# First attention: the context of half a pass is copied out of PSUM by ScalarE instead of VectorE

## What is computed

```python
scores = jnp.einsum('bhqd,bhkd->bhqk', q, k) / jnp.sqrt(HEAD_DIM)
scores = jnp.where(causal, scores, WHERE_CONST)
probs = jax.nn.softmax(scores, axis=-1)
ctx = jnp.einsum('bhqk,bhkd->bhqd', probs, v)
out = ctx @ Wo + bo
```

## Time and profile before

| | us |
|---|---|
| median of 3 runs (3386.05 to 3387.24) | 3386.67 |
| the profiled execution | 3384.95 |
| its span on the core | 3383.2 |
| span of the first attention, from its first exponential to the end of its last multiplication | 148.8 to 663.7 |
| one pass of it, from a copy of half 0 to the next (257.32 to 289.27) | 31.95 |

### The profile page before, as it was taken

One profiled execution on the slowest core, in us unless ns is written; L12 is line 12 of the kernel. 1 busy time (PEld: TensorE's weight loads), 2 busy tenths in 40 slices (PEclk: granted clock), 3 DMA queues, 4 the chain that ended last, 5 costly groups with the idle time before them and its releaser, 6 DMA issues. The chain is left out here.

```text
span 3383.2 us, 74549 instructions
## 1 busy us (share of the span) xinstructions
PE 2601.1 (77%) x23705; PEld 1456.7 (43%) x23705; DVE 2700.5 (80%) x8588; ACT 2383.1 (70%) x3987; POOL 2029.4 (60%) x4543
## 2 busy tenths in 40 slices
PE   3699999669654777777777777775777777758999
PEld 2233333234431444444444444443554454543444
DVE  5788888235438999999999999998999999744444
ACT  2266666533117999999999999997999999822221
POOL 3133333410117999999999999996999989640000
PEclk8699999879665777777778777877777777868999
DMA  5312211000121011001101100110110110010000
GB/s 150 94 47 53 55 49 40 14 25 26 52 63 21 2 18 18 11 9 18 18 2 18 18 12 9 18 18 2 18 18 2 18 18 2 2 33 3 7 7 10
DMA packets 115264, 85.87 MB, mean 25 GB/s; under 512 B 58153, under 2 KB 97339, under 8 KB 114875
## 3 DMA queue, kind: packets, MB, share of 16 engines
q1 hardware_dynamic: 106331, 75.20, 10.4%
q0 software_dynamic: 8192, 4.79, 0.9%
q10 hardware_dynamic: 352, 1.18, 0.1%
HBM read 54.25 MB, written 19.40 MB: 22 GB/s over the span
## 5 line engine op out<-in xcount | busy, mean ns | idle before, releaser
L1285 POOL TENSOR_TENSOR a_near<-a_side,a_z 128x1024 int32<-128x1024 int32 x512 | 968.9, 1892 | 42.6
L1181 PE MATMUL a_ST<-a_qs,a_ks 75*128 75x128 bf16 x4096 | 656.5, 249 | 397.5 <-DVE a_mask L1418 208.6
L1381 DVE MAX8 a_cand<-a_near 128x8 f32<-128x256 f32 x2048 | 810.8, 414 | 0.0
L1181 PEld LDWEIGHTS a_ST<-a_qs,a_ks 75*128 75x128 bf16 x4096 | 459.1, 114 | 564.1 <-DVE a_mask L1418 338.7
L1425 DVE TENSOR_SCALAR_CACHE_REDUCE a_z<-a_S,a_thr 128x1024 f32<-128x1024 f32 x512 | 650.2, 1270 | 33.6 <-POOL a_thr L1261 27.9
L1205 ACT ACTIVATE a_signs<-a_z,a_tiny 128x1024 bf16<-128x1024 f32 x512 | 589.6, 1152 | 73.9 <-DVE a_z L1425 72.4
L1198 ACT ACTIVATE a_signs<-a_S,search 128x1024 bf16<-128x1024 f32 x512 | 572.2, 1118 | 24.3 <-PE a_S L1136 24.2
L1220 ACT ACTIVATE a_eT<-a_ST 128x1024 f32<-128x1024 f32 x512 | 520.2, 1016 | 18.0 <-PE a_ST L1182 17.5
L776 ACT ACTIVATE a_eT<-a_ST 128x512 f32<-128x512 f32 (+3 forms) x768 | 329.2, 489 | 210.0 <-PE a_ST L761 148.6
L1136 PE MATMUL a_S<-a_ks,a_qs 72*128 72x512 bf16 x1024 | 394.4, 475 | 101.4 <-DVE a_z L1425 76.6
L880 DVE TENSOR_REDUCE a_mx<-a_S 128x1 f32<-128x512 f32 (+3 forms) x768 | 381.2, 547 | 77.3 <-PE a_S L748 67.7
(11 more groups left out here) (341 smaller groups left out, 4639.6 us busy)
## 6 DMA issues: line engine op xcount, KB each, us to landing
a_qs<-q_parts SPq DMA_DIRECT2D x174, 64.0 KB
a_ks<-k_parts SPq DMA_DIRECT2D x174, 64.0 KB
a_qs<-a_flip SPq DMA_DIRECT2D x512, 0.8 KB
q_parts<-p_qp SPq DMA_DIRECT2D x48, 128.0 KB, 1.7
k_parts<-p_kp SPq DMA_DIRECT2D x48, 128.0 KB, 1.8
a_qs<-q_parts SPq DMA_DIRECT2D x60, 96.0 KB
a_ks<-k_parts SPq DMA_DIRECT2D x60, 96.0 KB
f_w<-L_ffn_W SPq DMA_DIRECT2D x16, 256.0 KB, 2.8
```

Source lines behind the costliest of these rows:

```text
L1181: pe.matmul(ST[:, block_of], ks[:, base(hl) + kb * P:base(hl) + (kb + 1) * P], qs[:, tile(hl):tile(hl) + P], start=True, stop=False)
L1285: pool.tensor_tensor(near[:, hl % NEARS, :].bitcast(I32), side[:, one].bitcast(I32).broadcast_to([P, SEQ]), z[:, hl % H, :].bitcast(I32), ...
L1381: mm = dve.max(found[:, 8 * g:8 * g + 8], near[:, h2 % NEARS, g * SW:(g + 1) * SW])
```

## The change

The copy of `O` into `num` leaves DVE's program and enters ACT's, in the same slots: ACT makes the exponential of slot 19 (or 3), then the copy, with the same waits, then the exponential of slot 20 (or 4). The last copy of the last pass stands behind all exponentials. The operation is an `ACTIVATE` with the function Copy instead of a `tensor_copy`. Nothing else is changed.

```diff
         @block.scalar
         def _(act):
             def slot(it, p):
+                gi = p // G
                 if live(it):
-                    hf, kb, lo, hi = GROUPS[p // G]
-                    gi = p // G
+                    hf, kb, lo, hi = GROUPS[gi]
                     act.wait_ge(sturn_s, it * NB_ + (p + 1))
                     if p % G == 0 and not (isinstance(it, int) and it == 0 and gi < 4):
                         act.wait_ge(pv, it * NG + (gi - 3))
                     act.activation(eT[:, gi % 4, p % G, 0:hi - lo], ST[p % TURNED][:, 0:hi - lo], ACT.Exp, scale=SCALE0).then_inc(e_done, 1)
+                for at, hf, y in ((COPY1, 1, before(it)), (COPY0, 0, it)):
+                    if p == at and live(y):
+                        act.wait_ge(pv, NG * y + (FIRST_HALF if hf == 0 else NG))
+                        if not (isinstance(y, int) and y == 0):
+                            act.wait_ge(ctx_s, 2 * y + hf)
+                        act.activation(num[:, hf, :], O[:, :], ACT.Copy).then_inc(oc, 1)
...
             with act.Fori(1, ITERS) as it:
                 for p in range(NB_):
                     slot(it, p)
+            for p in range(COPY1 + 1):
+                slot(ITERS, p)
...
         @block.vector
...
-                for at, hf, y in ((COPY1, 1, before(it)), (COPY0, 0, it)):
-                    if p == at and live(y):
-                        dve.wait_ge(pv, NG * y + (FIRST_HALF if hf == 0 else NG))
-                        if not (isinstance(y, int) and y == 0):
-                            dve.wait_ge(ctx_s, 2 * y + hf)
-                        dve.tensor_copy(num[:, hf, :], O[:, :]).then_inc(oc, 1)
```

## The result

The changed kernel takes 3392.23 us (median of 12 runs, 3388.36 to 3394.56), the kernel before 3385.41 (12 runs, 3383.53 to 3389.42): a ratio of 1.0019, 95% interval 1.001 to 1.0028. It is some 7 us slower; 3.4 us faster was forecast. The profiled execution took 3390.81, its span is 3389.1.

What follows compares the result with a forecast made beforehand. PE was taken as the bound in the middle of the first attention, waiting 20.3 us for the copy. Terms 5.1 - 0.7 - 1.1 + 0.1 = 3.4 us, so 3386.67 - 3.4 = 3383.3 us; range 3380.2 to 3387.5.

Steps and rivals of the forecast that it cites:

- What is left, 0.04: Stages after the first attention: they start some us earlier and could see clock or DMAs fall otherwise; chance 0.04, no size.
- Copy on ACT: First attention, copy of half 0 (slot 19): 0.596 us on ACT, PE starts 0.43 us earlier, 6.5 us over fifteen places.
- Slot 3: First attention, copy of half 1: ACT is as late as DVE, 0.05 us lost 14 times, 0.7 us in all.
- Passes that maxima hold: First attention: in six of fourteen full passes late maxima limit the gain to margins of 0.13 to 0.40, together 1.24 us.
- slots 19 and 3: Copies of both halves in the first attention: slot 19 gives 5.1 us, slot 3 loses 0.7 us.
- Last pass: End of the first attention: both copies now lie on the path, 0.5 to 0.58 us two times, 1.1 us lost.
- Sum inside the stage: First attention: 5.1 - 0.7 - 1.1 + 0.1 = 3.4 us less.
- The whole pass moves along: First attention: gather and POOL's work shift with PE, all 15 places give 0.47, 6.0 us less, 3380.6; chance 0.13.
- The denominators hold all: First attention: all but the first and last places lose their gain, 0.8 us slower, 3387.5; chance 0.15.
- The copy dearer on ACT: First attention: each 0.1 us more per copy costs 3.1 us at up to 31 places; chance 0.14.
- PE waits for the exponential anyway: First attention, slot 19: the change does not do what it says, no size given; chance 0.02.

Runs made afterwards that it cites:

- run 1: Changed kernel plus a GpSimd memset of 128x5500 behind its last wait of the first attention, delaying later stages: 3399.11 us.
- run 2: Changed kernel plus a GpSimd memset of 128x3660 behind its last wait of the first attention, delaying later stages: 3396.32 us.
- run 3: Kernel before plus a GpSimd memset of 128x5500 behind its last wait of the first attention, delaying later stages: 3390.02 us.
- run 5: Changed kernel plus one one-column memset on VectorE behind its last work of the first attention: 3383.70 us, ratio 0.999 to the kernel before.
- run 6: Changed kernel plus two one-column memsets on VectorE behind its last work of the first attention: 3384.06 us, ratio 0.9997 to the kernel before.
- run 7: Changed kernel plus three one-column memsets on VectorE behind its last work of the first attention: 3383.78 us, ratio 0.9991 to the kernel before.
- run 9: Changed kernel plus four one-column memsets on VectorE behind its last work of the first attention: 3382.49 us, ratio 0.9987 to the kernel before.
- run 13: Changed kernel plus one copy of one number on ScalarE behind its last work of the first attention: 3398.10 us, ratio 1.0028.
- run 14: Kernel before plus 111 one-column memsets on VectorE behind its last work of the first attention: 3401.40 us, ratio 1.0037.
- run 18: Kernel before plus 47 one-column memsets on VectorE behind its last work of the first attention: 3398.74 us, ratio 1.0035.
- run 12: Kernel before with only the copy of half 0 moved to ScalarE, that of half 1 left on VectorE: 3383.92 us.

## Why the prediction was wrong

**The step that failed** is the one after the sum: "What is left, 0.04, is for stages after this one, which start some us earlier and could see their clock or DMAs fall otherwise." It had no price, so the sum went on as if nothing behind the first attention could change. It did change, by 10 us, and through neither clock nor DMAs nor the earlier start (runs 1 to 3). Moving the copies took 17 instructions out of VectorE's program, and put the unchanged code of the second attention at a place at which one instruction in 384 (16 tiles) is issued 0.34 us late. Shown for it: one to four idle instructions behind the change take the holes away (runs 5, 6, 7, 9), an instruction more on ScalarE doesn't (run 13), and the kernel before gets them without the change (runs 14, 18). Without the holes the changed kernel takes 3382.5 to 3384.1 us, where 3383.3 was forecast, and lies 2.4 to 5.1 us below the kernel before beside it, where 3.4 was.

**The terms of the sum**, against the profiled execution:
- *Copy on ACT.* Right but for the size of the gain. It starts 0.12 us before the exponential ahead of it ends (0.10 assumed), takes 0.61 (0.60), and the product comes 0.14 later, the upper end of 0.06 to 0.14:
```profile
286.42 0.59 ACT L776 ACTIVATE a_eT<-a_ST 128x512 f32<-128x512 f32 x1
286.89 0.61 ACT L782 ACTIVATE a_num<-a_O 128x512 f32<-128x512 f32 x1
...
287.64 1.07 PE L725 MATMUL a_O<-a_eT,a_vx 128*32 128x512 f32 x8 [0.45 <-ACT a_num L782]
```
  The wait of 0.84 became 0.45: a place gives 0.39, not 0.43, and the first of the fifteen only 0.30. This is the term that was mis-sized inside the stage.
- *Slot 3.* Right: 0.61 where 0.55 stood, a loss of 0.06 against 0.05 taken.
```profile
309.35 0.61 ACT L782 ACTIVATE a_num<-a_O 128x512 f32<-128x512 f32 x1
...
310.10 1.07 PE L725 MATMUL a_O<-a_eT,a_vx 128*32 128x512 f32 x8 [0.61 <-ACT a_num L782]
```
  In run 12, with this copy left on VectorE, a pass that nothing holds takes 31.56 us in place of 31.63.
- *Passes that maxima hold.* Right in kind, and in sum partly by luck. Passes take 31.63 where nothing holds them (255.26 to 286.89 below), and up to 32.36 where a maximum does (286.89 to 319.25):
```profile
255.26 0.60 ACT L782 ACTIVATE a_num<-a_O 128x512 f32<-128x512 f32 x1
...
298.00 0.34 PE L742 MATMUL a_S<-a_ks,a_qs 64*128 64x384 bf16 x2 [0.56 <-DVE a_mx L888]
...
319.25 0.60 ACT L782 ACTIVATE a_num<-a_O 128x512 f32<-128x512 f32 x1
```
  The maximum holds 11 us after the copy, as forecast; of the fourteen full passes four lasted over 31.8 us, six had been expected to be held. Three of the four are among the six (those after the copies that stood at 289.27, 385.13 and 513.35); the one of 353.18 had been counted as free. And the pass of 417.09, the one that maxima did hold before (32.34 us), went free, which the prediction had not counted. Other profiles of the same copies show four or seven such passes (runs 9, 5 and 6). Together the fourteen took 444.52 us against 447.77, so 3.25 less, and the first place gave 0.30: 3.55, where slots 19 and 3 were to give 4.4.
- *Last pass.* 1.18 us lost against 1.1; its two waits are 0.68 us each.
- *Sum inside the stage.* 2.3 us won (means over the runs: 500.5 us with both copies on VectorE at their old slots, 498.1 with both on ScalarE), against 3.4. The 3.3 that the profiled pair shows at the last copy look better than they are, by the 0.9 of the earlier start. A size off by about 1 us, below what the total can show.

**The rivals.** The whole pass moves along: no, passes were held. The denominators hold all: no. The copy dearer on ACT: no, 0.60. PE waits for the exponential anyway: no, it waits for the copy, 0.45. All four stayed inside the stage. The one that decided lay outside it, and the range of 3380.2 to 3387.5 was made without it.

**What stays open.** Why that place is slow. The traces show when the front of VectorE is late, not why. What they show beside it: VectorE's code of 8 tiles is 192 instructions (without the marks), of which a taken branch (the flag check, 0.8 us behind the context write) skips some; the hole comes once in two such rounds, always at the same instruction, ahead of that branch. The Trainium skill, page Runtime: NRT & Kernel Launch (Instruction fetch mechanics), says that a sequencer streams its program by DMA, that crossing a block is mostly hidden, and that a taken branch breaks the sequential prefetch and can cost a stall. The position dependence fits the blocks. The branch isn't needed: run 14 has the same hole in a place without any, in the row of 111 equal memsets behind the first attention, ahead of the 107th:

```profile
656.52 2.43 DVE L909 MEMSET a_left<- 32x1 f32 x106
659.30 0.18 DVE L909 MEMSET a_left<- 32x1 f32 x5 [0.35 <-issue]
```

By the same count the 107th is number 64 of its block of 128, as the late writes are; the 43rd, number 0, shows nothing. So the beginning of a block is what comes late, if the chip's blocks lie so. That the other beginnings don't show would be because VectorE still has work ahead of them or waits there anyway; the context write is the first instruction behind a wait that has just ended. This is argued, not shown.

The same page of the Trainium skill has blocks of 256 instructions (16 KiB); in this trace one instruction queue moves such blocks, and the other one half of that (1.67 MB in 204 packets):

```profile
q8 instruction: 185, 3.03, 0.4%
q14 instruction: 204, 1.67, 0.2%
```

By these figures of the Trainium skill an instruction has 64 bytes, so the smaller packets hold 128, an estimate. It also tells whose they are: at 64 bytes, and without the marks, TensorE's compiled program is 3.03 MB, and those of the four other engines are 1.68 MB together. VectorE's code then comes in blocks of 128, the block in which +111 and -17 are one place.

## What to carry to other kernels

Where an edit is worth less than 0.3%, the place of all later code on the same engine is part of the edit: build it again with one to four idle instructions behind it before judging it, and compare stage by stage, not by the total. Here the same change read +0.2% or -0.1%, by one memset. Of 12 places tried three were bad, so the next few are likely to be good, though not sure to be. And when an engine waits for work that stands behind others in a queue, first try to move it up in that queue: two numbers changed (slots 17 and 2, 18 and 2 or 17 and 1) gave 8 to 9 us, where another engine gave 2 to 5 (runs 5, 6, 7, 9 and 12).

## What the hardware showed that was not expected

An unchanged stretch of unrolled code ran 0.5% slower (1964 against 1954 us) by its place in VectorE's program alone, and the same hole of 0.35 us stood in a row of memsets. In the trace it shows as a constant idle time of 0.33 us ahead of one instruction, labelled "issue", or with an engine that has nothing to do with it. Delaying the stage by 3 to 5 us changed nothing in it. The granted clock of the stage read 0.76 in the changed kernel and 0.76 with the one memset more, and 0.77 both in the kernel before and in run 13, which has the holes: the lower mean over the span was no cause.
